# Attention's output projection in a fused language model tower: tokens or features on partitions

## The reference

```python
h = tok(x)                                             # [16, 512, 128]
h = h + attn(layernorm(h), W_qkv, b_qkv, W_out, b_out)
h = h + ffn(layernorm(h), router_w, router_b, Wi, Wh, b, Wo, bo)

def attn(x, W_qkv, b_qkv, W_out, b_out):
    Q, K, V = split(x @ W_qkv + b_qkv)
    ...                          # 64 summary tokens, and a window of 17 around each other token
    return out @ W_out + b_out                         # the output projection

def ffn(x, ...):                 # top 2 of 8 experts for each token
    gates = xt @ Wi + h @ Wh + b
    i, f, g, o = split(gates, 4)
    c = sigmoid(f) * c + sigmoid(i) * tanh(g)
    h = sigmoid(o) * tanh(c);    y = h @ Wo + bo
```

## Time and profile before

| | |
|---|---|
| median of 3 runs | 2039.79 us (2036.4 to 2039.81) |
| the profiled execution | 2034.29 us |
| its span, first to last instruction | 2032.5 us |
| TensorE (PE) busy | 1916.0 us, 94% |
| VectorE (DVE) busy | 1675.7 us, 82% |
| ScalarE (ACT) busy | 1018.1 us, 50% |
| GpSimd (POOL) busy | 68.8 us, 3% |
| mean granted TensorE clock | 0.953 of full |

### The profile page before, as it was taken

The page is one execution under the profiler, slowest core; times in us unless marked ns, Lnnn a source line. Parts: engine busy times, 40 slices in busy tenths (PEclk is TensorE's granted clock), DMA queues, the critical chain, the costliest instruction groups (busy, mean ns, idle before and its releaser), DMA issues.

```text
span 2032.5 us, 32554 instructions
## 1 busy us (share of the span) xinstructions
PE 1916.0 (94%) x12858; PEld 1083.5 (53%) x12858; DVE 1675.7 (82%) x3208; ACT 1018.1 (50%) x1099; POOL 68.8 (3%) x43
## 2 busy tenths in 40 slices
PE   3558899999999999999999999999999999999997
PEld 2325455555555555555555556555555555555554
DVE  2558798888889889888888889888888888889886
ACT  3245645545455454644545464554545545454553
POOL 1000000000000000000000000000000000000000
PEclk9678999999999999999999999999999999999998
DMA  3011110101011010110101001010211101011010
GB/s 108 14 30 27 23 40 19 39 7 45 19 23 38 20 35 11 39 24 22 36 17 41 11 24 39 20 38 7 44 19 23 35 20 38 12 26 37 22 26 6
DMA packets 57246, 57.10 MB, mean 28 GB/s; under 512 B 7755, under 2 KB 52669, under 8 KB 57095
## 3 DMA queue, kind: packets, MB, share of 16 engines
q1 hardware_dynamic: 57094, 55.03, 11.6%
HBM read 39.51 MB, written 4.48 MB: 22 GB/s over the span
## 4 chain that ended last, share of the span: by engine, by line
PE 78%; DVE 13%; ACT 3%; issue 3%; DMA 2%; SPq 1%; POOL 0%; DVEq 0%; ACTq 0%
PE gates L471 53%; PE FA L418 4%; PE FA L406 4%; PE yp L481 3%; PE yp L483 2%; PE yp L482 2%; DVE h L960 2%; DVE C L949 2%; DVE tmp L940 1%; DVE xn L728 1%; DVE tmp L945 1%; PE FA L391 1%; PE FB L425 1%; SPq L258 1%; PE FB L424 1%
## 5 line engine op out<-in xcount | busy, mean ns | idle before, releaser
L594 ACT ACTIVATE tmp<-gates,bias_sb 128x1024 f32<-128x1024 f32 x512 | 568.9, 1112 | 738.4 <-PE gates L471 736.1
L471 PE MATMUL gates<-xm,wi_sb 128*128 128x512 f16 x3072 | 779.8, 392 | 7.2 <-DVE xm L920 5.2
L471 PE MATMUL gates<-Hs,wh_sb 128*128 128x512 f16 x2880 | 714.1, 385 | 0.0
L471 PEld LDWEIGHTS gates<-Hs,wh_sb 128*128 128x128 f16 x2880 | 287.1, 100 | 357.5 <-issue 31.2
L471 PEld LDWEIGHTS gates<-xm,wi_sb 128*128 128x128 f16 x3072 | 295.5, 101 | 340.1 <-issue 59.5
L960 DVE SCALAR_TENSOR_TENSOR h<-yp,wy,h 128x128 f32<-128x128 f32 x1024 | 285.4, 342 | 8.2 <-PE yp L483 8.2
L481 PE MATMUL yp<-wo_sb,Hs 128*128 128x128 f16 x1024 | 188.1, 221 | 22.5 <-DVE h L960 22.5
L931 DVE SCALAR_TENSOR_TENSOR Hs<-tmp,Hs 128x1024 f16<-128x1024 f32 x128 | 156.2, 1221 | 50.9 <-ACT Hs L603 49.9
L940 DVE SCALAR_TENSOR_TENSOR tmp<-tmp 128x1024 f32<-128x1024 f32 x120 | 148.2, 1235 | 56.6 <-ACT tmp L594 55.6
L599 ACT ACTIVATE tmp<-C 128x1024 f32<-128x1024 f32 x128 | 135.1, 1056 | 117.7 <-DVE C L949 116.5
L483 PE MATMUL yp<-wo_sb,Hs 128*128 128x128 f16 x1024 | 188.5, 222 | 0.0
(11 more groups left out here) (160 smaller groups left out, 1513.4 us busy)
## 6 DMA issues: line engine op xcount, KB each, us to landing
masks<-mask_scratch SPq DMA_DIRECT2D x128, 256.0 KB, 4.8
vz<-vwin SPq DMA_DIRECT2D x64, 112.0 KB, 2.3
out_dram<-h SPq DMA_DIRECT2D x16, 256.0 KB, 2.2
qbd<-attn SPq DMA_DIRECT2D x128, 28.0 KB, 1.9
C<-in_wi SPq DMA_DIRECT2D x1, 2048.0 KB, 11.1
C<-in_wh SPq DMA_DIRECT2D x1, 2048.0 KB, 15.8
xm<-in_wo SPq DMA_DIRECT2D x1, 512.0 KB, 14.3
ids<-in_x_ids SPq DMA_DIRECT2D x16, 32.0 KB, 4.8
```

The source lines that it names most:

```text
L471: last = mm(gates[:, slot, k * SEQ:(k + 1) * SEQ], w, v, start=(n < K), stop=(n >= len(seq) - K))
L594: A(tmp[:, gate, :], gates[:, g % 2, :], ACT.Tanh, bias=bias_sb[:, e, gate:gate + 1], scale=UNSCALE).then_inc(s_tanh, 1)
```

## The change

The projection has `wout_sb` as its weights and all 512 tokens as one moving operand, in f32, into `FA[:, 1, :]`, with features on partitions. There the bias is one number for each partition, so ScalarE adds it while it copies the result from PSUM to `xnT`. Four f32 transposes in the next slot bring it back to tokens on partitions in `FB`, where VectorE reads it as before. `moments2` on VectorE and all pieces behind it move back by one slot, on every engine; `MASKS_AT` = 29 and `XM_AT` = 30 stay. `b_out` is loaded as a column, one number to each of 128 partitions, and the row of ones, its memset and its count in `s_prep` go.

```diff
-    SP_AT = dict(ids=0, qbd=6, vz=8, rows=28)
-    PE_AT = dict(emb=1, xT=3, qkv=4, summary=7, window=8, feature=14, values=18, proj=21, x2T=23,
-                 logits=24, maskT=27, bias=29)
-    ACT_AT = dict(h=1, xT=3, qkv=4, split=5, summary=9, window=11, pr_hi=15, feature=16, x2T=23,
-                  choice=25, maskT=27)
+    SP_AT = dict(ids=0, qbd=6, vz=8, rows=29)
+    PE_AT = dict(emb=1, xT=3, qkv=4, summary=7, window=8, feature=14, values=18, proj=21, projT=22,
+                 x2T=24, logits=25, maskT=28, bias=30)
+    ACT_AT = dict(h=1, xT=3, qkv=4, split=5, summary=9, window=11, pr_hi=15, feature=16, proj=21, x2T=24,
+                  choice=26, maskT=28)
...
-                  moments2=21, xn2=22, x_lo=24, choice1=25, choice2=25, weights=26, bias=30)
+                  moments2=22, xn2=23, x_lo=25, choice1=26, choice2=26, weights=27, bias=31)
...
-            (bout_sb[:, :], row(b_out)), (ident[:, :], ident_dram), (hones[:, :], head_ones), (band_sb[:, :], band),
+            (bout_sb[:, :], col(b_out)), (ident[:, :], ident_dram), (hones[:, :], head_ones), (band_sb[:, :], band),
...
                 if t == PE_AT["proj"]:
                     pe.wait_ge(S["attn"], b1)
+                    mm(FA[:, 1, :], wout_sb[:, :], attn[:, :], start=True, stop=True).then_inc(S["projT"], 1)
+                if t == PE_AT["projT"]:
+                    pe.wait_ge(S["projS"], b1)
                     for i in range(TILES):
-                        mm(FB[:, i * D:(i + 1) * D], attn[:, i * P:(i + 1) * P], wout_sb[:, :], start=True, stop=False)
-                        last = mm(FB[:, i * D:(i + 1) * D], ones1[:, :], bout_sb[:, :], start=False, stop=True)
+                        last = nc.tensor.transpose(FB[:, i * D:(i + 1) * D], xnT[:, i * P:(i + 1) * P], ident[:, :])
                     last.then_inc(S["proj"], 1)
...
+                if t == ACT_AT["proj"]:
+                    act.wait_ge(S["projT"], b1)
+                    A(xnT[:, :], FA[:, 1, :], ACT.Identity, bias=bout_sb[:, 0:1]).then_inc(S["projS"], 1)
...
-            V.memset(ones1[:, :], 1.0).then_inc(s_prep, 1)
```

More of the change, by code:

```diff
@@ L142, in lm_tower_kernel @@
         bo_sb = sb("bo_sb", [E, D])
-        bout_sb = sb("bout_sb", [1, D])
-        ones1 = sb("ones1", [1, P])
+        bout_sb = sb("bout_sb", [P, 1])
         ident = sb("ident", [P, P])
@@ L224, in lm_tower_kernel @@
             pw sw mw dw ew rw iw ow owr ow_c pf sf mf df ef rf if_ uf S mS dS eS rS iS prT O of0 of1
-            khi vhi qhi qlo klo vlo pn phi plo cf attn proj h2 bnst2 bnag2 veps2 rstd2 xn2 x2p xhi x32 xlo lgp lg m1 eq1 ix1 im1 k1 l2 m2
+            khi vhi qhi qlo klo vlo pn phi plo cf attn projT projS proj h2 bnst2 bnag2 veps2 rstd2 xn2 x2p xhi x32 xlo lgp lg m1 eq1 ix1 im1 k1 l2 m2
             eq2 ix2 im2 k2 dd ed sd w0 w1 wa wb wt mwc mwp mrow wT mout bp h2b wys"""
@@ L241, in row, with col @@
             return ap.rearrange("(a n) -> a n", a=1)
+        def col(ap):
+            return ap.rearrange("(n a) -> n a", a=1)
         consts = [
@@ L499, in _ @@
             pe.wait_ge(s_zero, 1)
-            pe.wait_ge(s_prep, 4)
+            pe.wait_ge(s_prep, 3)
             for t in range(NG * E):
@@ L536, in front @@
                 if t == ACT_AT["qkv"]:
-                    act.wait_ge(s_prep, 4)
+                    act.wait_ge(s_prep, 3)
                     act.wait_ge(S["qp"], b1)
```

## The result

The changed kernel takes 2055.47 us (median of 20 runs, 2036.43 to 2068.68), the kernel before 2039.29 us beside it (20 runs, 2030.64 to 2047.59): a ratio of 1.0066 with a 95% interval of 1.0046 to 1.0086. The ratio leaves out two executions of the changed kernel, 2067.10 and 2068.68 us, as slow ones. It is slower. The forecast was no change, 2038.5 us; the upper end of its range, 2054, is passed too.

The account below looks back on a forecast made before the run. The mask chain through VectorE at the step's end, not TensorE's own work, was taken to set the time after the change. -2.1 + 2.4 - 1.8 + 0.2 = -1.3 us from 2039.8 gave 2038.5 us, range 2022 to 2054.

Parts of the forecast that it names:

- Part 1: TensorE at the projection: one wide f32 matmul and four transposes replace 16 passes, saving 1.98 us a step.
- Part 2: VectorE's chain to the mask: second `cell` 2.7 us earlier, but ScalarE's mask copy 0.73 us later against the projection.
- Part 3: Last `unit_y` of each step: masks set its start, TensorE waits some 2.4 us; -0.15 us a step, -2.1 in 14.
- the race: At each step's end: TensorE's own work against an `add_y` queued behind the masked input's mask DMA; nearly even before.
- Part 4: TensorE's clock after the projection: five falls, some 1.7 us each, most expected gone, already counted in the mean.
- Part 5: First step and prologue: +2.4 us in step 0, -1.8 in the prologue, +0.2 for the `b_out` load.
- (a): TensorE is the bound and its last `unit_y` does not wait for the masks anyway: 2010 us; chance 0.07.
- (b): ScalarE's mask copy comes 0.5 to 1.2 us earlier than forecast: 7 to 17 us less, 2023 to 2033; chance 0.16.
- (d): The wide f32 matmul takes as long as the four it replaces, 1.65 us; time as forecast; chance 0.05.
- (c): Clock falls after the recurring wait before the last `unit_y`: 2046 at a third of steps, 2062 in all; chance 0.22.

Follow-up runs that it names:

- the first profile of the changed kernel: Profiled execution of the changed kernel, nothing else altered: 2043.4 us, span 2041.6 against 2032.5 us for the kernel before.
- the second: The changed kernel unaltered, measured and profiled again on another chip beside the kernel before: 2060.46 us, ratio 1.0114.
- filling it: Changed kernel with six unused 512-column matmuls (1.3 us) in the wait before the last `unit_y`: 2045.8 us, ratio 1.005; on an earlier chip 2036.29, 1.0006.
- the slots caught up: Changed kernel with choices, `weights`, `maskT`, `rows` and `bias` in their old slots: 2013.33 us, ratio 0.9889; with window and values stages cut too, 1973.08, 0.9682.
- the cut kernels: Window and values stages each split in half over two slots: kernel before 2011.98 us, ratio 0.9874; changed kernel 2008.77 us, ratio 0.9856.
- the padded changed kernel: Changed kernel with six more 512-column matmuls (1.3 us) in slot 12 of each step: 2065.53 us, ratio 1.014.

## Why the prediction was wrong, point by point

**Part 1 held.** The matmul and the transposes take 0.91 + 0.44 = 1.35 us between gates (predicted 1.30), the copy lies under the gates of slot 22.

**Part 2 held**, and it was the step on which most depended. Predicted and measured, from the projection on: residual add 3.99 and 4.14; second `cell` 19.71 and 19.85; wait before `maskT` 0.6 and 0.39; mask copy 26.65 and 26.75. The first excess of 0.15 is the only one of size, and it is passed on.

**Part 3 held for the race** (`unit_y` at 36.22 predicted, 35.6 to 36.8 measured, mean 35.94, as the masks came 6.78 us behind their copy and not 7.16; the wait of 2.4 at 1.5 to 2.6) **and failed in its last part**: "What follows, up to the next projection, is the same work from the same start." It is the same work, but not at the same clock. The window and values stages stand there, and I had not looked at the clock over them, although 20 of the 25 falls of before are there, and only five are those behind the projection that part 4 counts. Taken as unchanged, at 0, this term measured +15.1 us in the first profile of the changed kernel and +33.0 in the second, both against the one profile of before, over the 13 stretches from a last `unit_y` to the next projection. The 13 stretches ahead of it, from the projection to the last `unit_y`, got 5.7 and 5.9 us shorter, where the forecast of -0.15 us a step makes 2. Against the sum of -1.3 the medians are off by 17 and 26 us.

**Part 4 held as far as it went.** No fall stands behind a projection of after. It stopped at the one place where the change touches TensorE, while the falls changed at two stages that it does not touch.

**Part 5** was off by a little: step 0 +1.25 (predicted +2.4), prologue -1.89 (predicted -1.8 + 0.2; VectorE idles 4.06 us there, before 5.95; the issue of `b_out` costs 0.33 us, not 0.43). Neither reaches the loop: the first gates of step 0 run at half clock up to 127.2 us in both kernels, the first projection in the loop is 0.50 us later than before, and the first full step starts at 312.00 against 312.05. So the +0.8 us of this part came out at nothing.

**The rivals.** (a) and (b) did not come about: the copy was late as forecast. (The 2023 to 2033 of (b) is counted from 2039.8; from the forecast it would be 2022 to 2032.) Nor did (d): the wide matmul took 0.91 us and not 1.65. (c) was right in sign and in the kind of cost, not in its place: it put the falls behind the wait, in a third of the steps or in all; the two profiles have one and two of 14. Its 2046 to 2062 happens to span the result, but by another mechanism, so that is luck. The range was too narrow above, as it counted (c) up to 8 falls and had no case for falls elsewhere. The Trainium skill, "TensorE: Matmul & The Clock Gate", section "HAM oscillation — how this bites in real kernels", tells of a kernel whose wait for data, of about 3 to 5 us, recurs with each tile, and whose clock falls each time. The waits here are shorter, 1.45 to 2.79 us in the two profiles, so "that of all 14 steps" is more than the page bears out; one and two falls followed. Part 4 of the page has it that transposes do not count as busy in the same way; no step has a fall right behind the projection's four, but 0.44 us of them is little to test it by.

**What stays open.** What sets the place in a stage at which the clock falls; why a step with two double falls is mostly followed by another, and one with a single fall by its like; what brings a run into the one or the other, since runs of one kernel differ by 32 us; what part the wait has in it, and what filling it leaves (1.005). Shown is that the falls at the two sparse stages are the loss, and that cutting these stages removes it.

## What to carry to other kernels

Before the clock is taken as unchanged, look at the granted clock over one whole period of the loop, not only at the part that the change touches; where falls stand in the kernel before, a small change of the period can double them, so their doubled price belongs in the range. In a kernel like this one, try cutting long stages of narrow matmuls and laying the parts between wide ones: that alone gave 1.3%, and 3.2% together with the new projection and the slots caught up. When a piece moves by one slot, list for each engine what stands ahead of it in the new slot; here a `split_hi` of 1 us ahead of a copy of 0.57 made that copy 2.2 us later.

## What the runs showed of the hardware

TensorE's clock falls although the profile shows it busy all through: 84 matmuls of 32 columns back to back, 2.00 of each 2.00 us, and the clock goes from 0.99 to 0.50. The same matmuls in two lots of 42, 3.3 us of gates and `unit_y` between them, leave it at 1.00, but for three falls in the two profiles of the cut kernels. The Trainium skill, "TensorE: Matmul & The Clock Gate", section "A second HAM failure mode: psum-queue depth-cycling", tells of a clock that goes up and down where TensorE idles in small pauses between groups of matmuls. That is near to this case and not the same: the profile shows no pause within the stage, though it only models where matmuls end.

Waits alone are a poor sign: 3.49 us without a fall once and 3.56 (in the padded changed kernel) with one, 2.04, 2.08, 2.39, 2.62 and 2.79 us with one, and most of 1.5 to 2.4 us without. And added work may be nearly free: 19 us of matmuls cost 5 us in the changed kernel, 15 in the one before. A median of three runs of such a kernel can be off by more than the change: the changed kernel's runs lie between 2036 and 2069 us, those of its cut version, four of them, within 3.4.
